# Row stores of the last step's turns issued by ScalarE, and zero products in bf16, in a two-layer graph network

## What is computed

```python
h = jnp.maximum(_layernorm(x), 0.0)                  # x: what layer 0 left
l0, l1 = linear(h, W_l1_0, W_l1_1)                   # for the sources
si0, si1 = linear(h, W_si0, W_si1)                   # for the node itself
w = relu(edge_length_embedded @ W_fc1 / sqrt(10)) * sqrt(2) @ W_fc2 / sqrt(100)
y0, y1 = l0[edge_src], l1[edge_src]
m0 = w0 * y0 * e0
m1 = (w1 * y0)[:, :, None] * e1[:, None, :]
m2 = (w2 * e0)[:, :, None] * y1
m3 = w3 * einsum('eud,ed->eu', y1, e1) / sqrt(3)
s0, s1, s2, s3 = (segment_sum(m, edge_dst) / 4 for m in (m0, m1, m2, m3))
out = si + 0.5 * (s @ W_l2) * a / sqrt(96)
x = x + out
```

## Time and profile before

| | |
|---|---|
| median of three runs | 2381.24 us (2380.62 to 2384.26) |
| profiled execution | 2395.86 us, its span 2394.1 us |
| TensorE's mean granted clock in it | 0.97 of 2.4 GHz |
| TensorE, ScalarE, VectorE, POOL busy | 91%, 81%, 80%, 64% of the span |
| layer 0's last turn (204) ends; its record ends | about 1528 us; 1565 us |
| layer 1's last turn ends; its record ends | 2373.6 us; 2394.1 us |

### The profile page before, as it was taken

How to read it: one execution, slowest core, us unless ns; L and a number is a source line. 1 busy time by engine, 2 the same in 40 slices (tenths; PEclk the granted TensorE clock), 3 DMA queues, 4 the chain that set the end, 5 groups by cost and what they waited for, 6 DMA issues and landing times. The chain is left out here.

```text
span 2394.1 us, 79209 instructions
## 1 busy us (share of the span) xinstructions
PE 2184.4 (91%) x22003; PEld 2050.8 (86%) x22004; DVE 1907.2 (80%) x8636; ACT 1929.9 (81%) x5167; POOL 1528.5 (64%) x1925
## 2 busy tenths in 40 slices
PE   0899998999999999999999999569999998999997
PEld 0788888889888999899999999468999998999996
DVE  6878898789888889888889888237777776777775
ACT  2677888788888888798889989348888886888885
POOL 4866787678777887777777776144545554555551
PEclk9999999899999999999999999679999999999998
DMA  5455557644444445444444443256777775777773
GB/s 156 99 144 146 140 148 185 184 124 129 126 125 127 125 128 134 116 132 132 132 130 132 132 126 113 68 135 171 189 188 179 194 192 157 182 193 187 188 192 90
DMA packets 498819, 351.30 MB, mean 147 GB/s; under 512 B 188108, under 2 KB 484030, under 8 KB 498382
## 3 DMA queue, kind: packets, MB, share of 16 engines
q1 hardware_dynamic: 401007, 209.61, 34.2%
q0 software_dynamic: 41472, 69.42, 12.9%
q10 hardware_dynamic: 55904, 67.22, 8.1%
HBM read 199.00 MB, written 151.77 MB: 147 GB/s over the span
## 5 line engine op out<-in xcount | busy, mean ns | idle before, releaser
L1066 POOL DMA_INDIRECT xg<-table,from_row x411 | 397.4, 967 | 428.9 <-DVE msg L1239 225.4
L1628 PE MATMUL out_ps<-w_out,aggT 128*128 128x128 f32 (+1 forms) x4932 | 602.5, 272 | 19.4 <-issue 12.2
L1628 PEld LDWEIGHTS out_ps<-w_out,aggT 128*128 128x128 f32 x4932 | 589.4, 194 | 23.7 <-issue 18.8
L1066 POOL DMA_INDIRECT xg<-in_x,win x411 | 473.1, 1151 | 139.7 <-issue 120.3
L1613 PE MATMUL agg_ps<-sel,msg 128*128 128x128 f32 x3708 | 527.3, 284 | 28.9 <-issue 10.5
L1613 PEld LDWEIGHTS agg_ps<-sel,msg 128*128 128x128 f32 x3708 | 465.1, 196 | 38.2 <-issue 29.1
L1444 ACT ACTIVATE msg<-pw,win 128x64 f32<-128x64 f32 x1233 | 341.7, 353 | 5.2 <-issue 2.8
L1455 ACT COPY aggT<-agg_ps 128x768 f32<-128x768 f32 (+1 forms) x310 | 247.3, 798 | 111.4 <-PE agg_ps L1613 63.6
L1489 ACT ACTIVATE kept<-out_ps,a_sb 128x320 f32<-128x320 f32 x410 | 193.7, 524 | 51.3 <-PE out_ps L1657 39.3
L1410 ACT ACTIVATE hn<-xn,nmr,rs 128x192 f32<-128x192 f32 x411 | 201.3, 540 | 39.3 <-DVE nmr L1171 37.6
L1079 POOL TENSOR_TENSOR rs<-ve,neghalf 128x4 f32<-128x4 f32 x206 | 221.5, 1075 | 17.2
(11 more groups left out here) (194 smaller groups left out, 5047.7 us busy)
## 6 DMA issues: line engine op xcount, KB each, us to landing
base_tab<-kept ACTq DMA_DIRECT2D x205, 320.0 KB
kept<-base_tab SPq DMA_DIRECT2D x205, 320.0 KB
xn<-in_x SPq DMA_DIRECT2D x411, 80.5 KB, 1.8
table<-kept SPq DMA_DIRECT2D x410, 80.0 KB
out<-kept SPq DMA_DIRECT2D x410, 80.0 KB
ee_sb<-ee_parts SPq DMA_DIRECT2D x411, 22.5 KB, 1.7
ee_parts<-part SPq DMA_DIRECT2D x45, 196.0 KB
ee_sb<-ee_parts SPq DMA_DIRECT2D x411, 18.0 KB
```

The source lines that it names most:

```text
L1066: pool.indirect_dma_start(out=xg[:, t.slot, j, 0:D], out_offset=None, in_=edge_rows, in_offset=bass.IndirectOffsetOnAxis(ap=at, axis=0)).t ...
L1628: ins = pe.matmul(rows[0:NT, j, c0:c1], aggT[:, t.half, j, k, :], w[f"out{k}_"][:, :], start=fresh, stop=True, skip_group_check=not fresh)
```

## The change

The stores of turns 200 to 204 leave SyncE's `step` and are issued by ScalarE, in `store_last`, in both layers: in layer 0 one loop step earlier in the order than before, at T(8), behind the `base_tab` store of the same turn; in layer 1 at T(7), between `gates` and `copy_xw`. Since ScalarE has no registers with the window's addresses, it loads ten of them at turn 200. The semaphores that the stores add to are the same. The two zero products of a record read the same zeros as bf16 instead of f32.

```diff
+        last_nodes = [nc.scalar.alloc_register(f"last_node{k}") for k in range(LANES)]
...
-                if t := T(PRE + 1 if first else 7):
+                if (t := T(PRE + 1 if first else 7)) and t.n < NB - PER:
                     store_rows(t)
...
+            def store_last(t):
+
+                if t.n == NB - PER:
+                    lanes.known(act, t.at)
+                    act.load(last_nodes, plan_all[0:1, t.at, 0:LANES])
+                after_neighbour(act, t)
+                if not first:
+                    act.wait_ge(rows_ready, t.m + 1)
+                for j in range(PAIR):
+                    row = act.snap(last_nodes[t.lane + j], min_val=0, max_val=N) + (t.lane + j) * P
+                    act.dma_start(new_dram[bass.ds(row, P), :], kept[:, t.slot, j, 0:D]).then_inc(stored[t.slot], 16)
...
                     act.dma_start(base_tab[t.n], kept[:, t.slot, :, D:KEPT]).then_inc(stored[t.slot], 16)
+                if (t := T(PRE if first else 7)) and t.n >= NB - PER:
+                    store_last(t)
                 if t := T(2):
                     copy_xw(t)
...
+            zero_cols = zeros[:, 0:2 * P].bitcast(BF16)
...
-                pe.matmul(agg_ps[:, 0, 0:BLOCKS * NT], zeros[:, 0:P], zeros[:, 0:BLOCKS * NT], start=True, stop=False, skip_group_check=True)
+                pe.matmul(agg_ps[:, 0, 0:BLOCKS * NT], zero_cols[:, 0:P], zero_cols[:, 0:BLOCKS * NT], start=True, stop=False, skip_group_check=True)
...
-                pe.matmul(agg_ps[:, 0, 0:BLOCKS * NT], zeros[:, 0:P], zeros[:, 0:BLOCKS * NT], start=False, stop=True,
+                pe.matmul(agg_ps[:, 0, 0:BLOCKS * NT], zero_cols[:, 0:P], zero_cols[:, 0:BLOCKS * NT], start=False, stop=True,
```

More of the change, by code:

```diff
@@ L793, in one_layer @@
     deep = 1 if first else 2
-    edge_rec, long_tab, ee, regs = v["edge_rec"], v["long_tab"], v["ee_parts"][layer], v["regs"]
+    edge_rec, long_tab, ee, regs, last_nodes = v["edge_rec"], v["long_tab"], v["ee_parts"][layer], v["regs"], v["last_nodes"]
     nrow = ee.shape[0]
```

## The result

The kernel after took 2350.22 us in the median of four runs (2347.41 to 2357.62), the kernel before 2380.93 in four (2374.80 to 2384.26): ratio 0.9886, 95% interval 0.9854 to 0.9919, so 27 us less (19 to 35); the two medians are 30.7 us apart, and this text goes by the ratios and their intervals throughout. The prediction had 14.5 us less and a range that ended at 2361.5. The direction was right, the size was not. Before looking for a cause in the change, it pays to cut both profiled executions (spans 2394.1 and 2355.8 us) into stages, at the starts of rows that both have: ScalarE's scaling of turn 200 and its last normalization of node rows in layer 0, TensorE's first product of layer 1, VectorE's new rows of turns 0, 20 and 204 there.

The account below looks back on a forecast made before the run. TensorE bounds both main loops, left unchanged; the serial waits at each layer's end count. Gains of 6.2 + 6.4 + 1.9 = 14.5 us off the 2381.24 us median gave 2366.7 us, range 2361.5 to 2373.5.

Parts of the forecast that it names:

- The sum of the ends: Both layers' ends and records: gains of 6.2, 6.4 and 1.9 us, 14.5 us in all.
- layer 0's end: Layer 0, last turns to the record: node rows' normalization starts near 1534.8 instead of 1541.01, gain 6.2 us.
- Layer 1's end: Layer 1, last turn to the end: the record's chain starts earlier, product at 2378.65 instead of 2385.07, gain 6.4 us.
- The zero products: Closing product of each layer's record: one bf16 pass instead of two f32 passes, gain 0.97 us a layer.
- SyncE's loads: Record loads in layer 1: right behind turn 204's sums, at about 2370.4 instead of 2378.39.
- the 1514 that I named: Layer 0's end: time near which SyncE's loads of the record should be seen.
- A pair of stores: ScalarE's two 80 KB stores per turn in both layers' last turns: 1.06 us a turn, SyncE's price.
- turn 200's load and pair: ScalarE, both layers: register load 0.8 us plus pair, 1.86 us; covered in layer 0, 0.2 us over in layer 1.
- the first rival: ScalarE's stores or register load dearer than SyncE's, or layer 1's gather held up: 2369 to 2373 us, chance 0.14.
- The second rival: Another wait holds the record's loads; only issue time and zero products save: 4.1 us, 2377 us, chance 0.05.
- the third rival: ScalarE's queue backs up behind its own 320 KB stores: 7.5 us lost, 2389 us, chance 0.03.
- fourth: Layer 0's record: clock still or again at 2.4 GHz, its products lose 4 us: 2362.5 us, chance 0.05.

Follow-up runs that it names:

- the added traffic: Kernels before and after, each with SyncE copying 80 KB more in every turn of both layers: 2518.92 us and 2514.07 us.
- the two variants of ScalarE's queue: Kernel after with ScalarE's registers loaded once, early in layer 0 (0.9945 of before); the same with SyncE keeping turns 200 and 201's stores there (0.9962).
- l1_only: Kernel before with ScalarE's stores in layer 1 alone, zero products still f32: 2292.57 us, 0.9986 of the kernel before.
- a_again: Kernel after, unchanged, measured again on the faster chip: 2281.85 us, 0.9946 of the kernel before.
- a_again4: Kernel after, unchanged, measured again on the faster chip beside its two parts: 2280.66 us, 0.9937 of the kernel before.
- mix: Kernel after with ScalarE's registers loaded once, early, and SyncE keeping the stores of turns 200 and 201 in layer 0: 2283.95 us, 0.9962 of before.
- a_load: Kernel after with SyncE copying 80 KB more in every turn of both layers: 2514.07 us, 1.0482 of the kernel before.
- b_again3: Kernel before, unchanged, run again for a profile on the slower chip: span 2403.5 us.
- l0_only2: Later repeat, on the faster chip, of the kernel before with ScalarE's stores in layer 0 alone: 2286.51 us, 0.9966 of the kernel before.
- b_again2: Kernel before, unchanged, run again for a profile on the faster chip: 2297.77 us.

## Why the prediction was right or wrong

**The sum of the ends was right.** Over the profiles, without the added traffic and the two variants of ScalarE's queue: layer 0's end takes 31.5 us on average in nine profiles without ScalarE's stores there and 25.6 in seven with them, 5.9 us (forecast 6.2). Layer 1's end takes 21.8 us in the eight profiles in which nothing of it is changed and 15.5 in both of l1_only, 6.3 us (6.4). (The l1_only kernels lose 1.1 us of it ahead of that stage, as told above. The five profiles of the kernel after don't, and have 14.6 us with the zero product: 7.2 less, again 6.3 + 0.9.) The zero products give 0.9 us a layer (0.97). That is 14.0 us, forecast 14.5. On the faster chip the whole time moved by 12.4 us (a_again) and 14.5 us (a_again4).

**Its steps.** SyncE's loads came 0.19 us behind turn 204's sums in layer 1. In layer 0 the features were asked for at 1502.41, 1.8 us behind turn 200's scaling; the 1514 that I named is 2.9 us behind it in the kernel before, since that row itself came 10.5 us earlier in the profile after. A pair of stores cost ScalarE 1.1 us a turn, and turn 200's load and pair were covered (but for layer 1 in the l1_only kernels), so the first rival (a dearer ScalarE) is out, although the load took 1.0 and 1.5 us where I took 0.8; with the clock falling later its cover shrinks to nothing (TensorE waited 0.19 us for that copy in a_again4). The second rival, by which only issue time is saved, is out with it: ten stores less on SyncE gave 12 us in the two layers, most of it waiting in front of other loads. The Trainium skill, "DMA: Bandwidth & Descriptors", section "Issuing engines are not separate DMA queues", says that starting DMAs on several engines only saves the time it takes to initiate them. By that alone the gain would be the second rival's 4.1 us. The trace doesn't agree: what went is waiting in the order of SyncE's queue, 6.4 us in layer 1. No run here measures the engines' bandwidth. ScalarE's queue didn't back up as the third rival has it: of the kernel after's stores in five profiles the longest took 0.63 us, though single ones took 1.04 us in mix, 1.25 in a_load and 2.20 in l1_only. The clock was low for all or nearly all of layer 0's record in each profile (fourth); where it was at 2.4 GHz for about 3.4 us of it (b_again3, l0_only2) the record took 23.1 and 23.0 us instead of 24.3. One term was sized on an unusual row: the earlier trace rows has the clock at 2.4 GHz through turn 201, the only time but one. From turn 200's scaling to the normalization the forecast was 1534.8 - 1511.1 = 23.7 us; it was 26.6 in the first profile, in which turn 201 alone took 7.78 us instead of 5.24, and 25.2 to 25.3 in the others of the kernel after. So the profiled pair shows 3.3 us at layer 0's end, and pairs with the same clock 6.5. Without the two profiles of late fall, both without ScalarE's stores, the averages above give 6.3 instead of 5.9.

**The step that failed** is the last of the sum: "the median of the runs shown is 2381.24, 14.6 us under the profiled one, but both ends of layers are latency, so I take the same difference off it", with its spread, "the median of three runs moves by a microsecond or so". It took all between the ends as a constant. On the slower chip it isn't: in the profiled pair the loops, put at no change, went down by 27 us beside 10.9 of the ends and the record, the runs of the kernel before lie 46 us apart in one comparison (2381.8 to 2427.6) and 32 in another, and the change gave 27, 9 and 21 us in three measurements (0.9886, 0.9961, 0.9912); the intervals of the first two barely overlap, at 0.9918 to 0.9919. That profile already had the sign of it: it was 14.6 us over the median of its own kernel, and 9 pairs of turns in it alternate 6.1 and 3.1 us. A range of 12 us was far too narrow for it.

**What stays open** is whether on the slower chip the change is worth more than its ends. For it: two of the three measurements lie well over the ends' gain, and the table's loops are shorter on average in the three profiles of the kernel after (to turn 200 of layer 0 by 11 us, turns 0 to 20 by 8, turns 20 to 204 by 7). Against it: the first of these stretches holds nothing of the change, single profiles of one program differ there by nearly as much (1511.1 and 1521.0 before, 1500.6 and 1508.3 after), those of turns 20 to 204 overlap (699.4 before, 701.1 after), one program shows both patterns of layer 1's start, single runs of the kernel after also lie 34 us apart (2371.1 to 2405.6), and under added traffic the loops were no shorter. Drift would do it, and so would some effect of the program's layout on its timing; neither was isolated.

## What to carry over

A queue's cost is what its in-order waits hold up behind them. Before giving such work to another engine, find the engine with idle time at that point and count its pace there; here 1.1 us a turn on ScalarE, hidden in layer 1 and not in layer 0, bought an end 6 us shorter in each. A part taken alone can cost more than in the whole: layer 1's stores without layer 0's had one of 2.2 us in front. And before forecasting a median to a microsecond from one profile, look whether that profile is a usual one: how far it stands from the median, whether turns of a regular loop are regular, and whether the clock in it is the usual one.

## What the runs showed that I had not expected

**One program, two kinds of chip, some 85 to 100 us apart.** Chip 4 was of the faster kind in both comparisons that ran on it. 500 us of layer 1's loop, columns as above: in b_again2 (span 2296.0)

```profile
1700.00:2200.00 500.00, 500.00 (x4287) 494.67 (x4287) 420.34 (x1572) 454.22 (x1573) 289.33 (x287) 1.00 0.80 202
```

and in b_again3 (span 2403.5):

```profile
1700.00:2200.00 500.00, 477.71 (x3861) 461.86 (x3860) 377.88 (x1414) 415.52 (x1414) 247.86 (x257) 0.98 0.72 183
```

TensorE is busy throughout in the one and waits 22 us in the other, with a tenth fewer instructions done. From layer 1's first product to turn 0's new rows it is 15.0 us against 23.9. I called it slow memory in the expectations, and that isn't shown: a lone gather of 128 rows takes 2.59 us in a_again and 2.52 in the kernel after, and the bytes moved for a given DMA share are the same (202 GB/s at 0.80, 183 at 0.72). What VectorE and ScalarE wait for in the slow turns the trace only calls "remote".

**When the clock falls matters more than the change itself in one stretch.** Turn 201 of layer 0 takes 5.24 to 7.78 us, by a clock that fell 8.3 to 1.6 us behind the scaling of turn 200.
